# A macaron layer on one core: the order of ScalarE's and VectorE's instructions in an attention step

## What is computed

```python
x = x + 0.5 * ffn(layernorm(x))      # fp4-quantized linears 256 -> 704 -> 256, silu gate
x = x + attn(layernorm(x))
x = x + 0.5 * ffn(layernorm(x))
```

```python
q = (elu(q) + 1 + FEAT_EPS) / sqrt(E);  k = elu(k) + 1 + FEAT_EPS
kv_cumsum = cumsum(einsum('blhe,blhf->blhef', k, v), axis=1);  k_cumsum = cumsum(k, axis=1)
num = einsum('blhe,blhef->blhf', q, kv_cumsum)
den = einsum('blhe,blhe->blh', q, k_cumsum)[..., None] + FEAT_EPS
out = (num / den) @ Wout.T + bout
return (out - mean(out)) / sqrt(var(out) + LN_EPS) * gamma + beta
```

## Time and profile before

| | us |
|---|---|
| median of 3 runs | 2185.19 (2185.08 to 2187.68) |
| the profiled execution | 2185.49 |
| its span in the profile | 2183.1 |

### The profile page before, as it was taken

The page is one execution under the profiler, slowest core; times in us unless marked ns, Lnnn a source line. Parts: engine busy times, 40 slices in busy tenths (PEclk is TensorE's granted clock), DMA queues, the critical chain, the costliest instruction groups (busy, mean ns, idle before and its releaser), DMA issues.

```text
span 2183.1 us, 90488 instructions
## 1 busy us (share of the span) xinstructions
PE 2100.8 (96%) x30384; PEld 1503.3 (69%) x30384; DVE 2044.3 (94%) x5231; ACT 1926.2 (88%) x4136; POOL 1907.3 (87%) x3002
## 2 busy tenths in 40 slices
PE   3899999999999999999999999969999999999998
PEld 1566666666666688888888888855666666666665
DVE  7999999999999789999999999979999999999997
ACT  7888888888888789999999999978988888888885
POOL 5999999999999778888888888868999999999996
PEclk9999999999999999999999999989999999999999
DMA  4665555555555432222232222224555555555555
GB/s 103 131 125 115 116 115 116 115 115 115 114 114 108 84 58 61 61 61 61 61 62 62 61 61 61 62 44 76 120 116 114 114 114 114 114 115 115 115 118 118
DMA packets 719855, 208.72 MB, mean 96 GB/s; under 512 B 666400, under 2 KB 719520, under 8 KB 719776
## 3 DMA queue, kind: packets, MB, share of 16 engines
q1 hardware_dynamic: 719776, 207.76, 46.6%
HBM read 20.38 MB, written 16.78 MB: 17 GB/s over the span
## 4 chain that ended last, share of the span: by engine, by line
PE 89%; issue 3%; POOL 3%; DVE 3%; DMA 1%; ACT 1%; SPq 1%; POOLq 0%; DVEq 0%; ACTq 0%
PE ffn_ps_gu L861 39%; PE ffn_ps_down L873 20%; PE attn_ps_qk L1265 8%; PE attn_ps_sc L1310 5%; PE attn_ps_num L1297 4%; PE attn_ps_v_second L1278 4%; PE attn_ps_z L1333 3%; PE attn_ps_num L1302 2%; PE attn_ps_kT_first L1273 1%; PE attn_ps_z L1330 1%; PE attn_ps_kT_first L1321 1%; DMA attn_xT<-attn_x_hl 1%; POOL ffn_h_hl L791 1%; DMA x_sb<-in_L_ffn_w_up 0%; POOL ffn_h_hl L792 0%
## 5 line engine op out<-in xcount | busy, mean ns | idle before, releaser
L861 PE MATMUL ffn_ps_gu<-wgu_hi,ffn_xT 128*128 128x512 f16 (+1 forms) x3072 | 737.7, 363 | 18.4 <-DVE ffn_hx L710 8.0
L861 PEld LDWEIGHTS ffn_ps_gu<-wgu_hi,ffn_xT 128*128 128x128 f16 x3072 | 300.7, 98 | 304.7 <-issue 22.3
L861 PE MATMUL ffn_ps_gu<-wgu_lo,ffn_xT 128*128 128x512 f16 (+1 forms) x1536 | 431.0, 362 | 0.0
L791 POOL TENSOR_TENSOR ffn_h_hl<-ffn_q,ffn_h_scale_hi 128x704 f16<-128x704 f16 x256 | 352.4, 1376 | 28.0 <-DVE ffn_q L751 8.6
L807 ACT ACTIVATE ffn_quarter<-ffn_y,offsets 128x960 int16<-128x960 f32 (+2 forms) x264 | 282.5, 1070 | 99.3 <-DVE ffn_y L759 96.9
L873 PE MATMUL ffn_ps_down<-wd_hi,ffn_hT 128*128 128x256 f16 x2816 | 349.3, 273 | 8.1 <-DVE x_sb L735 4.2
L792 POOL TENSOR_TENSOR ffn_h_hl<-ffn_q,ffn_h_scale_lo 128x704 f16<-128x704 f16 x256 | 355.1, 1387 | 0.0
L873 PEld LDWEIGHTS ffn_ps_down<-wd_hi,ffn_hT 128*128 128x128 f16 x2816 | 274.6, 98 | 68.8 <-issue 7.1
L721 DVE TENSOR_REDUCE ffn_per_block<-ffn_hx 128x60 f32<-128x960 f32 (+2 forms) x264 | 298.1, 1129 | 5.3
L759 DVE TENSOR_TENSOR ffn_y<-ffn_hx,ffn_per_block 128x960 f32<-128x960 f32 (+2 forms) x264 | 292.6, 1108 | 0.0
L843 ACT ACTIVATE ffn_odd<-ffn_quarter,offsets 128x960 f16<-128x960 int16 (+2 forms) x264 | 278.8, 1056 | 10.8 <-POOL ffn_shift L786 10.8
(11 more groups left out here) (184 smaller groups left out, 5246.3 us busy)
## 6 DMA issues: line engine op xcount, KB each, us to landing
x_sb<-in_L_attn_x SPq DMA_DIRECT2D x128, 128.0 KB, 2.4
out<-x_sb SPq DMA_DIRECT2D x128, 128.0 KB, 2.1
attn_v_eo<-attn_v_nat SPq DMA_DIRECT2D x256, 34.0 KB, 1.8
ffn_xT<-ffn_x_hl SPq DMA_TRANSPOSE x256, 2.5
ffn_hT<-ffn_h_hl SPq DMA_TRANSPOSE x256, 3.5
attn_xT<-attn_x_hl SPq DMA_TRANSPOSE x128, 2.4
attn_oT<-attn_o_hl SPq DMA_TRANSPOSE x128, 2.5
x_sb<-in_L_ffn_w_gate SPq DMA_DIRECT2D x2, 352.0 KB, 5.0
```

The source lines that it names most:

```text
L791: nc.gpsimd.tensor_tensor(blocks(h_hl[par][:, 0:INNER]), blocks(q[par][:, 0:INNER]), over_block(h_scale_hi[par][:], HB), ALU.mult)
L861: last = nc.tensor.matmul(ps_gu[par][:, a:b], xT[par][:, c, :], w[:, k, a:b], start=(n == 0), stop=(n == len(terms) - 1))
```

## The change

On ScalarE, k's copy of chunk i now stands directly behind the Relu, then comes the exponential, and v's copy comes third. The second of the two own copies of v is moved behind xn. As v's copy is now the later of the two, TensorE waits for v_nat of chunk i + 1 ahead of the kv products, and no longer for k_nat of chunk i (in the last step, which has no next chunk, it still waits for k_nat). In step 0 TensorE also waits for v_nat of chunk 0 before it makes v of chunk 1.

On VectorE, zg is made directly behind the two aggregations, then comes the addition to x, then before. zg becomes a pair of buffers, so that it can be made ahead of the addition that still reads the one of the step before. The waits that zg had on the addition and the addition had on zg are gone.

```diff
@@ attention: buffers
-        zg = sb("zg", [P, D])
+        zg = pair("zg", [P, D])
@@ vector_step, behind both aggregations
+            if valid(tz, N):
+                ready(dve, "z_stats", tz)
+                nc.vector.scalar_tensor_tensor(zg[oth][:], ps_z[:, 0:D], mv[oth][:, 2:3], rows[:, 1, :], ALU.subtract, ALU.mult).then_inc(S["z_gamma"], 1)
             if valid(ta, N):
                 ready(dve, "x_beta", ta)
                 dve.wait_ge(S["rstd"], ta + 7)
-                ready(dve, "z_gamma", ta)
-                nc.vector.scalar_tensor_tensor(x_sb[:, ta, :], zg[:], rstd[par][:, 1:2], x_sb[:, ta, :], ALU.mult, ALU.add).then_inc(attn_added, 1)
+                nc.vector.scalar_tensor_tensor(x_sb[:, ta, :], zg[par][:], rstd[par][:, 1:2], x_sb[:, ta, :], ALU.mult, ALU.add).then_inc(attn_added, 1)
@@ vector_step, behind "before"
-            if valid(tz, N):
-                ready(dve, "z_stats", tz)
-                if valid(ta, N):
-                    dve.wait_ge(attn_added, ta + 1)
-                nc.vector.scalar_tensor_tensor(zg[:], ps_z[:, 0:D], mv[oth][:, 2:3], rows[:, 1, :], ALU.subtract, ALU.mult).then_inc(S["z_gamma"], 1)
@@ scalar_step, behind the Relu
+            if valid(i, N):
+                ready(act, "kT_done", i)
+                freed(act, "kv_done", i, 1)
...
+                nc.scalar.activation(k_nat[:], ps_kT, ACT.Identity, bias=feat_eps[:]).then_inc(S["k_nat"], 1)
+            if valid(tf, N):
+                ready(act, "relu", tf)
+                nc.scalar.activation(expo[oth][:], expo[oth][:], ACT.Exp, scale=-1.0).then_inc(S["exp"], 1)
...
                 ready(act, "v_done", tf)
...
-                ready(act, "relu", tf)
-                nc.scalar.activation(expo[oth][:], expo[oth][:], ACT.Exp, scale=-1.0).then_inc(S["exp"], 1)
-            if valid(i, N):
-                ready(act, "kT_done", i)
-                freed(act, "kv_done", i, 1)
...
-                nc.scalar.activation(k_nat[:], ps_kT, ACT.Identity, bias=feat_eps[:]).then_inc(S["k_nat"], 1)
@@ scalar_step, the own copies of v
-                for a in range(2):
-                    last = nc.scalar.activation(v_eo[oth][half(a), a, a], v_nat[oth][half(a), a], ACT.Copy)
-                last.then_inc(S["v_own"], 1)
+                nc.scalar.activation(v_eo[oth][half(0), 0, 0], v_nat[oth][half(0), 0], ACT.Copy)
@@ scalar_step, behind xn
+            if valid(tf, N):
+                nc.scalar.activation(v_eo[oth][half(1), 1, 1], v_nat[oth][half(1), 1], ACT.Copy).then_inc(S["v_own"], 1)
@@ tensor_step, ahead of v
+                if isinstance(i, int) and i == 0:
+                    ready(pe, "v_nat", i)
@@ tensor_step, ahead of kv
-                ready(pe, "k_nat", i)
+                if valid(tf, N):
+                    ready(pe, "v_nat", tf)
+                else:
+                    ready(pe, "k_nat", i)
```

More of the change, by code:

```diff
@@ L918, in attention_constants @@
                      sb("feat_eps", [P, 1]), sb("keep", [P, N]))
-ATTN_PLACES = {"o": 8352, "oT": (1024, 2048), "o_hl": (9376, 4096), "mid": (5632, 6176), "before": (6720, 7264), "first": 7808, "second": 11264, "k_nat": 12352, "zg": 13376,
+ATTN_PLACES = {"o": 8352, "oT": (1024, 2048), "o_hl": (9376, 4096), "mid": (5632, 6176), "before": (6720, 7264), "first": 7808, "second": 11264, "k_nat": 12352, "zg": (13376, 3072),
                "k_eo": (15104, 17152), "scores": 19200, "v_nat": (23296, 24384), "v_eo": (25472, 27648), "q_feat": (29824, 30848), "q_rows": (31872, 33920),
@@ L1211, in scalar_step @@
                 nc.scalar.activation(expo[oth][:], ps_qk[:], ACT.Relu, bias=one[:], scale=unscale[:, 1:2]).then_inc(S["relu"], 1)
+            if valid(i, N):
+                ready(act, "kT_done", i)
+                freed(act, "kv_done", i, 1)
+                if isinstance(i, int) and i == 0:
+                    act.wait_ge(F["h_split"], N)
+                nc.scalar.activation(k_nat[:], ps_kT, ACT.Identity, bias=feat_eps[:]).then_inc(S["k_nat"], 1)
+            if valid(tf, N):
+                ready(act, "relu", tf)
+                nc.scalar.activation(expo[oth][:], expo[oth][:], ACT.Exp, scale=-1.0).then_inc(S["exp"], 1)
                 if isinstance(tf, int) and tf == 0:
@@ L1218, in scalar_step @@
                 nc.scalar.activation(v_nat[oth][:].rearrange("p a j w -> p (a j) w")[:, :, 0:E], blocks(ps_v), ACT.Copy, scale=unscale[:, 0:1]).then_inc(S["v_nat"], 1)
-                ready(act, "relu", tf)
-                nc.scalar.activation(expo[oth][:], expo[oth][:], ACT.Exp, scale=-1.0).then_inc(S["exp"], 1)
-            if valid(i, N):
-                ready(act, "kT_done", i)
-                freed(act, "kv_done", i, 1)
-                if isinstance(i, int) and i == 0:
-                    act.wait_ge(F["h_split"], N)
-                nc.scalar.activation(k_nat[:], ps_kT, ACT.Identity, bias=feat_eps[:]).then_inc(S["k_nat"], 1)
             if valid(tf, N):
```

## The result

The changed kernel takes 2193.54 us (median; 2192.94 to 2197.73), the kernel before beside it 2184.62 us (2181.15 to 2187.68): ratio 1.0047, 95% interval 1.0038 to 1.0057. It is 9 to 10 us slower; no change was forecast.

What follows compares the result with a forecast made beforehand. TensorE's own stream was taken to set the attention step. Steady steps 0 and start -0.1 turned the profiled 2185.49 into 2185.4 us; less 0.3 to the median, 2185.1 us, range 2177 to 2190.

Steps and rivals of the forecast that it cites:

- The term that was put at 0: VectorE's 0.05 us shift on the chain to xT's landing, over 32 turns 1.6 us up or down, taken as 0.
- two small waits: TensorE's waits ahead of num (0.23 us a step) and for xT (0.28 us in one step of four) would stay.
- The faster rival: ScalarE's slack and VectorE's shift shorten the xT and mask waits: 11.5 us, 2173.6; half, 2179; chance 0.28.
- ScalarE's order: Attention steps: exponential unmoved, v_done wait gone, moved own copy returns about 0.14 us; work unchanged within 0.05 us a step.
- ScalarE gets slack, the kernel nothing: ScalarE loses 0.05 us a step of waiting, but nobody who sets the end waits for it: no gain.
- the first rival: Same as the faster rival: ScalarE's slack reaches the xT chain through o's copy; up to 11.5 us faster, chance 0.28.
- kv behind v_nat: TensorE's kv products now wait for v's copy, released at 1206.80 instead of 1206.79; 0.29 us of cover, cost nothing.
- The rival with 2198 us: v_nat gates TensorE's kv products in every step; 0.1 us beyond the cover costs 12.8 us; chance 0.10.
- SyncE's copies of v: They wait for v_nat in the queue with both transposes; v_nat is 0.38 us ahead, cost nothing.
- the 2190 us rival: SyncE reaches its wait before v_nat, oT and xT slip: 3.2 us, 4.8 with VectorE's shift; chance 0.07.
- VectorE's order: zg starts 0.05 us late behind the aggregations, covered by 0.26 us of waiting at den, 0.36 on average.
- The first steps: First attention steps: exponential's table load 1.3 us earlier, but xT's landing limits the gain to 0.1 us.

Runs made afterwards that it cites:

- e9: Changed kernel plus one wait a step: VectorE's addition to x waits for GpSimd's first rstd instruction; 2185.35 us, 1.0011 of the kernel before.
- e6: Changed kernel with seven semaphore increments that nobody waits for ahead of VectorE's attention loop, shifting it in the list; 2189.81 us, 1.0032 of the kernel before.
- e1: Kernel before with only the ScalarE and TensorE part of the change, VectorE as before; 2185.32 us, 1.0013 of the kernel before.
- e2: Kernel before with only VectorE's new order and the pair of zg, ScalarE and TensorE as before; 2188.68 us, 1.0027 of the kernel before.
- e5: Kernel before with the pair of zg and without zg's wait on the addition, VectorE's order the old one; 2185.20 us, 1.0008 of the kernel before.
- e13: e9 with its VectorE loop shifted by seven instructions as in e6; ratio 1.0005 to the kernel before, 2183.86 us.
- e4: Changed kernel with one always satisfied wait a step ahead of zg, on the previous step's addition; 2183.46 us, 0.9999 of the kernel before.

## Why the prediction was wrong

The step that failed: "The addition no longer runs beside GpSimd's first rstd instruction but beside what follows that. No row shows that pairing. The nearest bound is the shift of VectorE itself, 0.05 us, ... 1.6 us up or down; I take 0". What follows is the power, and beside the addition it takes up to 0.28 us longer. The term that was put at 0 was the length of that instruction. The right bound stood in the trace: the first rstd instruction, which did run beside the addition, took 0.26 to 0.35 us in the kernel before and takes 0.19 to 0.22 in the changed one, so a GpSimd instruction of two columns could already be seen to vary by more than 0.05 us with its neighbour. The price was 0.19 us at shift, or 6.1 us over 32 turns (0.20 as a mean, 6.4 us). e9 gives back 8.2 us, because there shift comes 0.07 us earlier than even in the kernel before.

A second step failed with it: "num's late start hangs on the mask, VectorE's step between den and the aggregations, where nothing moves." VectorE's first instruction of the turn moved by 0.10 us, the mask behind it with it, and TensorE's wait ahead of num grew from 20.8 to 24.5 us. e6, where the hole is away, has 20.7.

By the prediction's steps:

- TensorE's stream sets the step, with two small waits left. Right in the kernel before. But a wait of TensorE "once a turn" is not only something to be won; it means that whatever is added on the chain behind it is paid in full. I counted 0.27 us at xT as a possible gain and didn't ask what a later rstd would cost there. The faster rival took that chain with one sign, and the slower ones had no more of it than the 1.6 us of VectorE's shift.
- ScalarE's order. The exponential keeps its place behind relu to 0.07 us (1.08 us before, 1.01 after), the v_done wait is gone, and k's copy takes the second place without waiting. v's copy has its reader 0.06 us behind its end (0.03 worked out). "Its 0.60 us need not run out" was wrong: in the changed kernel the own copy starts 0.63 us behind the start of xn (1207.98 to 1208.61), so the move gave nothing back.
- "ScalarE gets slack, the kernel nothing": right for the half alone within 0.13% (e1). In the changed kernel the moved own copy puts ScalarE's copy of o later, and GpSimd's split of o with it, 0.04 us a turn on the chain to xT. That is the path of the first rival, with the other sign. The changed kernel also exceeds e2 in TensorE's wait ahead of num, 24.5 us against 20.1. That is the mask's wait, which comes and goes with the hole (e6), though e2 has the hole without it: why the two meet only beside ScalarE's new order or VectorE's old one (e5) stays open. q_rows isn't it: ScalarE had it ready at 1205.22, and num started at 1205.90.
- kv behind v_nat: right. No idle row ahead of the kv products; in the changed kernel v's copy ended at 1207.12 and the products started at 1207.75. The rival with 2198 us had the sign, not the mechanism.
- SyncE's copies of v: nothing was seen of the 2190 us rival either. SyncE issues oT 0.23 us behind the end of GpSimd's split of o, and xT 1.46 us behind oT, in both kernels (1204.53 and 1205.99; 1210.66 and 1212.13, with rounding). xT is late because that split is late.
- VectorE's order: zg starts 0.21 us behind the start of the z aggregation, 0.20 worked out. The wait at den fell from 0.36 to 0.33 us a step, within the 0.31 to 0.36 named. All true, and beside the point: VectorE's own time was never at stake, its neighbour's was.
- The first steps. The table load stands right behind relu (its end, 747.74):
```profile
747.76 1.28 ACT L1218 ACT_TABLE_LOAD   x1
749.05 0.63 ACT L1218 ACTIVATE attn_expo<-attn_expo 128x512 f32<-128x512 f32 x1
```
From relu's start to the exponential's it is 2.09 us, and was 3.37: 1.28 less, and 1.3 was forecast. TensorE's next q and k (751.78) come 4.82 us behind that relu (746.96) and came 4.93 behind it (749.60 and 744.67): 0.1, as forecast.
- Not foreseen: with waits dropped from VectorE's list the hole at the top of the turn grows from 0.18 to 0.28 us. Taking it away is worth 0.09 to 0.10 us a turn in the traces of e6 and e13. In the executions e6 is 3.7 us below the changed kernel and e13 1.5 below e9, each within the intervals.
- Luck had no part: the time lies outside the range on the side of the rivals for slower, and neither of them names what happened.

The stated signs of being wrong ("a step other than 5.45 us on average", "the xT rows gone or doubled") caught it: a turn of four takes 21.98 us against 21.72 (means of 21 or 22 turns), 5.49 a step against 5.43, and the xT row is 1.6 times as long.

## What to carry to other kernels

When an instruction moves on VectorE, list what GpSimd has under way at its new place as well as what waits for it, and look for the length of the same GpSimd instruction beside different neighbours (its minimum, median and maximum show it). Where the bounding engine has even one wait per loop turn, follow the chain behind it to the end and price delays on it at full, with both signs. And a wait that is always satisfied is not free or harmless to drop: e4's single one took back all of the 0.47%, by 0.09 us of position beside GpSimd and by the hole that went with it.

## What the runs showed of the hardware that was not expected

- GpSimd's power on 128x2 took 0.70 us where no VectorE instruction with two inputs from SBUF held it, and up to 0.98 when VectorE's addition of two 128x256 operands from SBUF had started first; the hold ended 0.34 us after that start, and 0.21 us after the start of an instruction on 128x136.
- In the other order the power held nobody that the rows show: the addition took 0.48 us where it started 0.03 us (e4) or 0.18 us (e9) behind it. Behind GpSimd's split of x, on 255 columns, the addition took 0.53 us against 0.45 with GpSimd idle (kernel before).
- VectorE idled 6.2 us in 22 turns at the first instruction of its loop in the changed kernel; with the same loop seven places further on in the list it idled 3.7 us.
- With a loop body of eight steps instead of four the changed kernel took 2332 us instead of 2194, and 3.59 MB of instruction fetches instead of 0.64.
